# A two-layer graph network on one core: two counting groups of each tile moved next to their neighbours

## What is computed

```
edges = stack([src, dst])
h = relu(layernorm(x))
# layer 0: norm, relation-wise graph convolution, elu, projection
n = ln_weight * h * rsqrt(mean(h*h) + 1e-6)
z = n @ W_root + bias
for r in (0, 1):
    z += segment_sum((n[src] @ W_rel[r]) * (type == r), dst) / max(count_r(dst), 1)
x = x + h + elu(z) @ wo_weight
# layer 1: graph attention
g = relu(layernorm(x)) @ W
e = exp(-leaky_relu(al[src] + ar[dst]))         # al = g @ a_l, ar = g @ a_r
x = x + elu(segment_sum(e * g[dst], src) / (segment_sum(e, src) + 1e-5))
```

## Time and profile before

| what | us |
|---|---|
| median of 3 runs (lowest to highest) | 514.78 (514.48 to 515.09) |
| span of the profiled execution, first to last instruction | 513.4 |
| TensorE busy | 495.0 (96%) |
| VectorE busy | 374.9 (73%) |
| ScalarE busy | 226.6 (44%) |
| granted TensorE clock, mean | 0.998 of full speed |

### The profile page before, as it was taken

The page is one execution under the profiler, slowest core; times in us unless marked ns, Lnnn a source line. Parts: engine busy times, 40 slices in busy tenths (PEclk is TensorE's granted clock), DMA queues, the critical chain, the costliest instruction groups (busy, mean ns, idle before and its releaser), DMA issues.

```text
span 513.4 us, 7812 instructions
## 1 busy us (share of the span) xinstructions
PE 495.0 (96%) x2983; PEld 426.4 (83%) x2983; DVE 374.9 (73%) x644; ACT 226.6 (44%) x382; POOL 74.6 (15%) x72
## 2 busy tenths in 40 slices
PE   3999999999999999999999999999999999999995
PEld 2889989988988998898888888888888888888885
DVE  4846885599889999998955555557598877877623
ACT  5865443415966666668722222334133323322201
POOL 1362213100000000000000000000083333332300
PEclk9999999999999999999999999999999999999999
DMA  9972273404013235237911111000023322222211
GB/s 253 230 241 83 80 225 116 130 2 114 2 46 109 87 98 144 81 123 275 323 49 41 40 43 49 31 0 1 0 80 95 87 81 73 68 80 81 80 43 44
DMA packets 22186, 49.15 MB, mean 96 GB/s; under 512 B 4798, under 2 KB 10709, under 8 KB 22018
## 3 DMA queue, kind: packets, MB, share of 16 engines
q1 hardware_dynamic: 20879, 44.66, 29.5%
q10 hardware_dynamic: 1008, 3.67, 2.0%
q0 software_dynamic: 256, 0.26, 0.2%
HBM read 33.05 MB, written 16.85 MB: 97 GB/s over the span
## 4 chain that ended last, share of the span: by engine, by line
PE 89%; DVE 5%; ACT 3%; issue 1%; DMA 1%; ACTq 0%; SPq 0%; DVEq 0%
PE ps L1330 11%; PE ps L1595 9%; PE ps L1597 9%; PE ps L1596 9%; PE ps L1489 8%; PE ps L1577 7%; PE ps L1578 7%; PE ps L1576 7%; PE ps L1399 4%; PE ps L1548 2%; PE ps L1418 2%; PE ps L1550 2%; PE ps L1549 2%; PE ps L1562 1%; PE ps L1380 1%; PE ps L1374 1%
## 5 line engine op out<-in xcount | busy, mean ns | idle before, releaser
L1595 PE MATMUL ps<-h_hi,att_hi 125*125 125x512 f32 (+1 forms) x190 | 73.5, 387 | 0.0
L1596 PE MATMUL ps<-h_lo,att_hi 125*125 125x512 f32 (+1 forms) x190 | 72.6, 382 | 0.0
L1597 PE MATMUL ps<-h_hi,att_lo 125*125 125x512 f32 (+1 forms) x190 | 72.5, 382 | 0.0
L1576 PE MATMUL ps<-wg,gT_hi 128*125 128x512 f32 x160 | 63.7, 398 | 0.0
L1577 PE MATMUL ps<-wg,gT_hi 128*125 128x512 f32 x160 | 63.1, 394 | 0.0
L1578 PE MATMUL ps<-wg,gT_lo 128*125 128x512 f32 x160 | 63.0, 394 | 0.0
L1489 PE MATMUL ps<-msg_hi,adj_hi 125*125 125x288 f32 x180 | 50.2, 303 | 0.2 <-ACT adj_hi L596 0.2
L1489 PE MATMUL ps<-msg_lo,adj_hi 125*125 125x286 f32 x180 | 45.9, 295 | 0.0
L471 POOL TENSOR_TENSOR some<-first_att 125x625 f32<-125x625 f32 x1 | 2.4, 2440 | 276.4 <-DVE first_att L1159 276.4
L691 ACT ACTIVATE em<-ps,rinv 125x512 f32<-125x512 f32 (+1 forms) x21 | 14.0, 668 | 64.2 <-DVE hp L1203 64.2
L1597 PEld LDWEIGHTS ps<-h_hi,att_lo 125*125 125x125 f32 x190 | 35.2, 186 | 7.9
(11 more groups left out here) (215 smaller groups left out, 1116.8 us busy)
## 6 DMA issues: line engine op xcount, KB each, us to landing
xt<-in_x SPq DMA_DIRECT2D x10, 448.0 KB
xh_scratch<-xt SPq DMA_DIRECT2D x10, 448.0 KB
xt<-xh_scratch SPq DMA_DIRECT2D x10, 448.0 KB
x_scratch<-xt SPq DMA_DIRECT2D x10, 448.0 KB
x1t<-x_scratch SPq DMA_DIRECT2D x10, 448.0 KB
xr<-x_scratch SPq DMA_DIRECT2D x10, 448.0 KB
out_x<-xr SPq DMA_DIRECT2D x19, 224.0 KB
wg_raw<-in_L_gnn_W ACTq DMA_DIRECT2D x7, 512.0 KB, 7.4
```

The costliest lines, as they stand in the source:

```text
L1576: M.matmul(to, hi, wg[k][:, 0, cut], start=n == 0, stop=False)
L1595: M.matmul(to, hi[:, s, :], h_hi[:, s, cut], start=s == 0, stop=False)
L1596: M.matmul(to, hi[:, s, :], h_lo[:, s, cut], start=False, stop=False)
L1597: return M.matmul(to, lo[:, s, :], h_hi[:, s, cut], start=False, stop=s == TILES - 1)
```

## The change

TensorE runs `counted(t, 1)` directly behind `counted(t, 0)`, ahead of the first sum, and no longer between the two sums. It runs `counted(t, 3)` directly behind `counted(t, 2)`, ahead of the output's first half, and `counted(t, 4)` ahead of the last of the three transposes instead of behind it. ScalarE's list is put in the same order: the eviction of group 1 stands ahead of `y_split` (in round 2 ahead of `split_wo`), and the eviction of group 3 ahead of `elu`. VectorE, GpSimd and the DMA queues keep their lists.

```diff
 ScalarE
                 elu(*tile(0))
                 evicted(2, 0)
+                evicted(2, 1)
                 split_wo()
-                evicted(2, 1)
                 y_split(*tile(0))
                 turned(1, 0)
                 evicted(2, 2)
+                evicted(2, 3)
                 turned(1, 1)
-                evicted(2, 3)
+                evicted(2, 4)
                 turned(1, 2)
-                evicted(2, 4)
                 elu(*tile(1))
                 for t in range(3, TILES):
                     evicted(t, 0)
+                    evicted(t, 1)
                     y_split(*tile(t - 2))
-                    evicted(t, 1)
                     turned(t - 1, 0)
                     evicted(t, 2)
+                    evicted(t, 3)
                     elu(*tile(t - 1))
                     turned(t - 1, 1)
-                    evicted(t, 3)
+                    evicted(t, 4)
                     turned(t - 1, 2)
-                    evicted(t, 4)
 TensorE
                 for t in range(2, TILES):
-                    counted(t, 0)
+                    counted(t, 0, 1)
                     if t > 2:
                         y_transposed(*tile(t - 2))
                     summed(0)(*tile(t - 1))
-                    counted(t, 1)
                     if t == 2:
                         y_transposed(*tile(0))
                     summed(1)(*tile(t - 1))
                     turned(t - 1, 0)
-                    counted(t, 2)
+                    counted(t, 2, 3)
                     if t > 2:
                         output1(0)(*tile(t - 2))
                     turned(t - 1, 1)
-                    counted(t, 3)
+                    counted(t, 4)
                     turned(t - 1, 2)
-                    counted(t, 4)
                     if t == 2:
                         output1(0)(*tile(0))
                     output1(1)(*tile(t - 2))
```

## The result

| | us |
|---|---|
| changed kernel, median of 4 runs | 522.74 (522.66 to 523.18) |
| kernel before beside it, median of 4 runs | 514.93 (514.48 to 516.79) |
| ratio, 95% interval | 1.0146 (1.0129 to 1.0164) |
| span of the profiled execution | 520.9 (before 513.4) |

The change makes the kernel 1.5% slower. The forecast was 522.1, with a range of 519.0 to 523.6.

What follows compares the result with a forecast made beforehand. It took a closed loop through TensorE and VectorE to bound each round. Six rounds of 0.90 (5.40), 1.77 at the start and 0.14 at the end gave 7.3 us on 514.78: 522.1 us, range 519.0 to 523.6.

Steps and rivals of the forecast that it cites:

- a round: Counting stage, one z_of start to the next on VectorE: grows from 12.33 to 13.23 us, 0.90 more.
- group 1 alone: counted(t, 1) ahead of the first sum waits for VectorE's rows(t+1, 1): round of 12.79 us, 0.46 more.
- y_of behind z_of: elu behind a second eviction on ScalarE moves VectorE's y_of from 3.04 to 3.48 us after z_of, 0.44 later.
- round 2, longer by: split_wo behind an eviction of 1.16 us delays VectorE and counted(3, 1); z_of of round 3 comes 1.77 us later.
- behind the start of round 9's z_of, longer by: End of the counting stage: 0.14 us for transposes now behind the last counted group; no other wait seen.
- y_split: Group 1's eviction ahead of it on ScalarE leaves VectorE idle 0.63 us, with 1.19 of room: costs nothing.
- first rival: TensorE's own work is the limit and VectorE moves up with it: 2.3 us less, 512.5 us; chance 4%.
- second rival: The new wait of counted(t, 1) is there but elu's shift is hidden: 4.7 us more, 519.5 us; chance 14%.
- The third: Rival: the wait is filled, by rows in time or a free round 2: 515.4 us; chance 6%.
- the fourth: Rival: y_split becomes a limit too if the eviction pair runs later: 523.5 us and above; chance 10%.
- The rule on products in program order: TensorE pulls only weight loads ahead, so products queue behind the waiting group; if they could pass, the round would be 12.38.
- The rule on the busiest engine: Optimise the highest-occupancy engine first, by occupancy TensorE; not followed, because the loop runs through both TensorE and VectorE.

Runs made afterwards that it cites:

- g1_alone: Kernel before with only the moves of group 1 on TensorE and ScalarE; 520.16 us, ratio 1.0091, mean round 12.78 us.
- rows_ahead_of_y: Changed kernel with VectorE's rows(t+1, 0) and rows(t+1, 1) ahead of y_of in rounds 3 to 9; 517.63 us, ratio 1.0044.
- elu_ahead: Changed kernel with elu back ahead of the eviction of group 3 in rounds 3 to 9; 519.93 us, ratio 1.0096.
- g1_back_elu_ahead: Changed kernel with group 1 back between the sums and elu back ahead of the eviction of group 3; 515.96 us, ratio 1.0011.
- g1_back: Changed kernel with group 1 counted between the sums again and evicted behind y_split (round 2: behind split_wo); 516.13 us, ratio 1.0019.
- before_filled: Kernel before with only VectorE's list changed, rounds 3 to 9: rows(t, 4) ahead of z_of, rows(t+1, 0) ahead of y_of; 513.67 us, ratio 0.9972.
- after_filled: Changed kernel with VectorE's list changed: rows(t, 4) ahead of z_of, rows(t+1, 0) ahead of y_of; 518.05 us, ratio 1.0047.

## Why the prediction was right

*The place.* The forecast said that counted(t+1, 1), moved ahead of the first sum, would meet VectorE's last rows of the round, and that the wait would run in a circle through both sums, `s_ps`, z_of, elu, y_of and these rows. The distance from rows' end to the group is 0.14 to 0.15 in the changed kernel and in g1_alone; opening the circle at VectorE (rows_ahead_of_y) takes 0.81 of the 0.89 back with nothing else undone.

*The sizes.* Predicted and measured by the profiled executions:

| term | predicted | measured |
|---|---|---|
| a round | 13.23 | 13.22 |
| of it group 1 alone | 12.79 | 12.78 (g1_alone, elu_ahead) |
| y_of behind z_of | 3.48 | 3.48 |
| round 2, longer by | 1.77 | 1.74 |
| six rounds, longer by | 5.40 | 5.38 |
| behind the start of round 9's z_of, longer by | 0.14 | 0.76 |
| span | +7.3 | +7.5 |

The measured parts are 1.74 + 5.38 + 0.76 = 7.88; the stretch ahead of round 2 came out 0.38 shorter (129.88 against 130.26). That stretch is the same code; over all the runs here it lies between 129.8 and 131.3, so this and a part of the last term is scatter, and that the span came within 0.2 of the forecast owes something to luck: -0.38 ahead of round 2 stands against the 0.62 that the last term lacked.

*The term that was mis-sized.* "With 1.77 at the start and 0.14 for the transposes behind the last counted group": behind round 9 I had only the transposes. y_of of round 9 is late by the same 0.44 as the others, and the list of VectorE behind it has no idle time, so this too goes through. The last y transposes start 14.76 behind that z_of before (239.59 - 224.83) and 15.20 in the changed kernel:

```profile
246.77 0.48 PE L1531 MATMUL ps<-ident,yb 125*127 125x125 f32 x2 [0.63 <-DVE yb L1067]
...
252.98 0.48 PE L1576 MATMUL ps<-wg,gT_hi 128*125 128x512 f32 x1
```

The second layer's products start 20.96 behind it before (245.79 - 224.83), 21.41 here (252.98 - 231.57): 0.45 more. The experiments agree that this is elu's shift: 20.95 in elu_ahead, which takes it back, and 21.14 in g1_back_elu_ahead against 21.61 in g1_back. The 0.14 for the transposes is not to be seen in elu_ahead, which has them. I had written that I saw no wait behind the stage that gives something back; the step missing was to ask whether the lateness of y_of also leaves the stage. The other 0.3 is in the second layer, which took between 266.8 (before_filled, 511.4 - 244.62) and 268.6 (g1_alone, 519.9 - 251.34) in the runs here, with no order to it, so it says nothing.

*y_split.* Predicted idle 0.63 with room for it; measured 0.53, with 0.54 to 0.58 still idle ahead of the next z_of, and 0.81 in rows_ahead_of_y with a round of only 12.41. It was not the limit in the changed kernel.

*Span and median.* The forecast puts the median 1.4 us above the span. All runs for which both are known have 1.75 to 1.95 between them (the changed kernel: 522.66 and 520.9), so the execution that was profiled before, with its span of 513.4, was not the one of the median, and the 1.4 is not what lies around the first and the last instruction. The forecast of the median does not hang on it, since it adds 7.3 to the median itself.

*The rivals.* That TensorE's own work is the limit (first rival) falls with g1_alone: with one switch less between its sums and nothing taken from VectorE, each round grew by 0.45. But it was right in one thing: VectorE could be moved up, only by its own list and not by TensorE's; before_filled does that and gains 0.3%. The second rival, elu's shift hidden, falls with elu_ahead: taking the shift back shortens the rounds by 0.44. The third and the fourth (rows in time; y_split) did not occur in the changed kernel; in after_filled y_split did become part of the loop.

*The rule on products in program order.* In the changed kernel TensorE stood 0.86 us ahead of counted(t+1, 1) and issued none of the products behind it, though y_of, which the transposes need, was over at 195.98 and the last eviction of the tile, which the sums need, at 196.42. The Trainium skill (TensorE: Matmul & The Clock Gate, Part 2, Step-by-step: what each phase is for) says that products stay in program order; the trace agrees in a second place.

*The rule on the busiest engine.* The other rule weighed was to start with the engine of the highest occupancy (the Trainium skill, Perfetto Trace Analysis, Identifying the Most-Contended Engine). For TensorE the same section does not take the busy time of the products, which the forecast took, but the share of peak arithmetic that is reached and the share of the weight loads. By the second TensorE leads over the whole span (83% against VectorE's 73%), but in the stage the two stand level, 18.32 us against 18.52 of 20, so the rule does not single out TensorE here. before_filled left TensorE's list alone and gained 0.3% by a move on VectorE.

## What to carry to other kernels

When two engines are both nearly full in a stage (here 99% and 93% of the stretch read), an instruction moved up on one is worth what the other's list allows. Take the time at which its input is ready, not the time at which the instruction now runs, and if the input is the last thing of the other engine's round, look for the way back from the moved instruction to that round's start: a wait on such a circle is paid in every round. Before moving the consumer, see whether the producer has idle time ahead of a wait of its own that could hold the work, and check the last round by itself, since it lacks the work of the next one that covers its waits.

## What the runs showed that I had not expected

- Two waits were not additive in the way that their sizes suggest: with group 1 moved, elu behind a second eviction costs 0.44 us a round; with group 1 in its old place it costs 0.00 a round (12.44 against 12.45), with the same 0.35 us of idle on VectorE. Behind the last round it costs 0.46 and 0.47 in the two cases.
- Once VectorE was filled, the next bound lay close: settled rounds of 12.05 us on TensorE, 12.00 with the groups joined and 11.98 with elu later, with VectorE idle only 0.4 us a round (for the 16-bit copy of group 4) and TensorE without a wait in nearly all of them.
- after_filled closed a loop that spans two rounds, through y_split (24.8 us for two). The length of a round alternates there, and only the sum of two neighbours stays.
- The releaser that the list of waits gives for the new wait was wrong by coincidence: two ends 0.08 us apart (198.63 and 198.71), of which the code waits for the first.
